# Forty expert weighings on GpSimd begin one group earlier, behind a read-out instead of behind a semaphore

## The reference

```python
# sub-layer 1, a state-space layer (512 channels, 16 states each)
xb, z = split(rms_norm(x) @ in_proj_w)
xc = silu(causal_conv4(xb) + conv_b)
dt, Bm, Cm = split(xc @ x_proj_w)
dt = softplus(dt @ dt_proj_w + dt_proj_b)
h[t] = exp(dt * A) * h[t-1] + dt * Bm * xc      # per channel and state
y[t] = sum_over_states(h[t] * Cm)
y = ((y + xc * D) * silu(z)) @ out_proj_w + x

# sub-layer 2, a mixture of 16 experts (all computed, 4 weighed per token)
combine = top4_of_16_weights(x @ gate_weight)   # zero for the 12 others
act = silu(x @ gate_proj[e]) * (x @ up_proj[e])
y = sum_over_e((act @ down_proj[e]) * combine[:, e])
```

## Time and profile before

| What | Value |
|---|---|
| median of 3 runs | 2657.78 us (2655.29 to 2659.5) |
| time of the profiled execution | 2660.87 us |
| its span, first to last instruction | 2659.1 us |
| PE busy | 2385.4 us (90%) |
| DVE busy | 2418.0 us (91%) |
| ACT busy | 1606.2 us (60%) |
| POOL busy | 1495.1 us (56%) |
| mean granted TensorE clock | 0.957 |
| weighings L896 | 256, 1275 ns each |
| read-outs L911 | 256, 4529 ns each |

### The profile page before, as it was taken

The page is one execution under the profiler, slowest core; times in us unless marked ns, Lnnn a source line. Parts: engine busy times, 40 slices in busy tenths (PEclk is TensorE's granted clock), DMA queues, the critical chain, the costliest instruction groups (busy, mean ns, idle before and its releaser), DMA issues.

```text
span 2659.1 us, 26874 instructions
## 1 busy us (share of the span) xinstructions
PE 2385.4 (90%) x8416; PEld 1187.2 (45%) x8416; DVE 2418.0 (91%) x3097; ACT 1606.2 (60%) x3186; POOL 1495.1 (56%) x531
## 2 busy tenths in 40 slices
PE   5546899999989999898999989899999989898987
PEld 2112354544545454454545445454544545443554
DVE  4989999999999999999999999999999999999542
ACT  6556566665665666666665666666666665644331
POOL 0555565656555565656666565656656565665521
PEclk9768899999999999999999999999999999998999
DMA  4441433525353352534345253534435353442221
GB/s 144 155 145 50 161 130 116 175 87 188 106 154 119 118 183 88 188 108 151 123 133 166 87 188 111 159 112 138 161 94 181 114 161 100 147 149 84 80 71 58
DMA packets 172762, 344.50 MB, mean 130 GB/s; under 512 B 16044, under 2 KB 81357, under 8 KB 164173
## 3 DMA queue, kind: packets, MB, share of 16 engines
q1 hardware_dynamic: 164700, 334.93, 37.5%
q0 software_dynamic: 7920, 7.87, 2.2%
HBM read 291.35 MB, written 51.38 MB: 129 GB/s over the span
## 4 chain that ended last, share of the span: by engine, by line
PE 64%; DVE 20%; ACT 11%; issue 5%; DMA 1%; POOL 0%; SPq 0%; ACTq 0%; DVEq 0%; POOLq 0%
PE Gp L483 13%; PE MY L501 12%; PE Up L491 12%; DVE hs L1033 10%; PE FP L408 7%; PE Y L515 6%; DVE hs L1019 5%; PE FP L446 4%; PE FP L420 3%; PE FP L428 2%; ACT dA L591 2%; ACT XB L684 1%; ACT L591 1%; PE Y L512 1%; DVE th L1148 1%
## 5 line engine op out<-in xcount | busy, mean ns | idle before, releaser
L911 POOL TENSOR_TENSOR hs<-hs,Cb 128x2048 f32<-128x2048 f32 x256 | 1159.5, 4529 | 174.9 <-DVE hs L1019 174.9
L591 ACT ACTIVATE dA<-dtr,A 128x512 f32<-128x512 f32 x1024 | 696.7, 688 | 603.2 <-DVE hs L1033 601.8
L896 POOL TENSOR_TENSOR th<-th,cmb 128x512 f32<-128x512 f32 x256 | 325.5, 1275 | 945.8 <-DVE hs L1019 851.3
L1033 DVE TENSOR_TENSOR_SCAN hs<-dA,carry,hs 128x512 f32<-128x512 f32 x512 | 630.7, 1269 | 13.7 <-ACT dA L591 12.8
L1033 DVE TENSOR_TENSOR_SCAN hs<-dA,hs 128x512 f32<-128x512 f32 x512 | 598.8, 1208 | 37.5 <-ACT dA L591 37.0
L483 PE MATMUL Gp<-x2T,Wgu 128*128 128x512 f32 x1024 | 534.3, 646 | 82.2 <-DVE th L1143 81.6
L1019 DVE TENSOR_TENSOR hs<-dxr,Bb 128x2048 f32<-128x2048 f32 x256 | 587.8, 2296 | 6.9 <-DMA dxr<-dx_d 6.9
L491 PE MATMUL Up<-x2T,Wgu 128*128 128x512 f32 x1024 | 491.6, 603 | 0.0
L501 PE MATMUL MY<-Wdn,th 128*128 128x256 f32 x2048 | 484.4, 380 | 1.6 <-POOL th L896 1.6
L501 PEld LDWEIGHTS MY<-Wdn,th 128*128 128x128 f32 x2048 | 384.3, 190 | 135.1 <-issue 89.8
L483 PEld LDWEIGHTS Gp<-x2T,Wgu 128*128 128x128 f32 x1024 | 183.5, 198 | 420.0 <-issue 275.6
(11 more groups left out here) (168 smaller groups left out, 1798.5 us busy)
## 6 DMA issues: line engine op xcount, KB each, us to landing
dxr<-dx_d SPq DMA_DIRECT2D x128, 512.0 KB, 7.2
dtr<-dt_d SPq DMA_DIRECT2D x64, 1024.0 KB, 5.5
cmb<-cm_d SPq DMA_DIRECT2D x256, 256.0 KB, 3.6
Wdn<-in_w_dn SPq DMA_DIRECT2D x256, 128.0 KB, 3.4
Bb<-bc_d SPq DMA_DIRECT2D x64, 256.0 KB, 3.0
Cb<-bc_d SPq DMA_DIRECT2D x64, 256.0 KB, 3.6
dt_d<-XB SPq DMA_DIRECT2D x15, 1024.0 KB, 4.3
dx_d<-DX SPq DMA_DIRECT2D x15, 1024.0 KB, 5.8
```

The costliest lines, as they stand in the source:

```text
L591: act.activation(dA[h % 2][:, :], dtr[:, M % 2, beta, :], ACT.Exp, scale=A[:, k:k + 1]).then_inc(s_dA, 1)
L896: pool.tensor_tensor(th[:, q % NTH, :], th[:, q % NTH, :], cmb[:, q % 2, :], ALU.mult).then_inc(m_a, 1)
L911: pool.tensor_tensor(hs[:, G % NH, :, :], hs[:, G % NH, :, :], Cb[:, s, :].unsqueeze(1).broadcast_to([P, NBETA, CH]), ALU.mult).then_inc(s ...
L1033: dve.tensor_tensor_scan(hv, dA[h % 2][:, :], hv, first, ALU.mult, ALU.add).then_inc(s_h, 1)
```

## The change

Three groups, 6, 10 and 13, get a second look at the weighing, in periods up to 14. In them the weighing of the expert of group `G - 1` is written behind `read_out(G - 1)`, and the group behind (7, 11 or 14) then has none. That is one weighing in period 1 (group 13) and three in each of periods 2 to 14, forty in all.

```diff
+WEIGH_EARLY = (6, 10, 13)
...
                 if 0 <= G < NGRP:
                     pool.wait_ge(s_u, G + 1)
-                for q in experts_at(G - 2):
-                    weigh(q)
+                if g - 1 not in WEIGH_EARLY or p >= NC - 1:
+                    for q in experts_at(G - 2):
+                        weigh(q)
                 if 0 <= G - 1 < NGRP:
                     read_out(G - 1)
+                if g in WEIGH_EARLY and p < NC - 1:
+                    for q in experts_at(G - 1):
+                        weigh(q)
```

## The result

| What | Before | After |
|---|---|---|
| median of the runs | 2658.5 us (2655.29 to 2659.5, 4 runs) | 2688.86 us (2688.25 to 2689.88, 4 runs) |
| ratio, 95% interval | | 1.0117 [1.0102, 1.0131] |
| span of the profiled execution | 2659.1 us | 2688.1 us |
| mean granted TensorE clock | 0.957 | 0.952 |
| PE, DVE busy | 2385.4, 2418.0 us | 2400.4, 2437.9 us |

The account below looks back on a forecast made before the run. The chain gave PE 64% and POOL 0%, turning to DVE and ACT in groups 10 to 13. Direct 18.2 us plus 6.8 for clock falls made 25 on 2660.87, or 2686; 2682 us for the median, range 2662 to 2693.

Parts of the forecast that it names:

- L956 held in group 6: DVE's first `p_scale2` instruction in group 6 waits for the weighing, paying 0.84 us and delaying `inputs` of group 7.
- group 10, even and odd: In group 10 the weighing holds `f_dx`, on the chain: 0.43 us more in even periods, 0.84 in odd.
- group 12, even: In even periods `inputs` of group 12 no longer meets a read-out's tail, saving 0.11 us on the chain.
- direct sum: Costs over seven even and six odd periods, less the group 12 gain: 8.1 + 10.1 = 18.2 us.
- falls of the clock: After PE's idle time at period ends, 4.5 more drops of TensorE's clock at 1.5 us each: 7 us.
- What DVE meets: A DVE instruction begun during a weighing pays the weighing's end, less its own start, less 0.13 us.
- the clock falls in nearly every period: Rival: TensorE's clock drops at all thirteen period ends, 14 us on top of 18.2, giving 2690 us; chance 0.15.
- PE itself is hardly touched by it before group 10: Group 6's delay of 0.84 us costs PE only some 0.1 to 0.2 at `gate` of group 7.
- `f_dx` comes at about +8.15 and might win: Rival: in group 10 `f_dx` starts before the weighing and is not held; 2665 us, chance 0.23 in some or all periods.
- 0.2 us even: If `f_dx` goes first, group 6's delay costs about 0.2 us per even period, 0.5 per odd: 4.4 us.
- Faster: Rival: at period ends the clock drops vanish, saving 7 us, and DVE collisions are small; 2654 us, chance 0.05.
- nothing moves: Rival: the weighing might wait for `cmb` or `expert_up` and start late, so no effect; chance 0.07.

Follow-up runs that it names:

- e3: Only the weighing of group 13 moved early, against the kernel before; 2657.38 us, ratio 0.9996.
- e10: Kernel before with only group 13's weighing moved, plus four matmuls of zeros on PE at the end of group 13; 2651.39 us, ratio 0.9977.
- e4: Kernel after the change plus four matmuls of zeros on PE at the end of group 13 of periods 2 to 14; 2668.07 us.
- e5: Kernel before the change plus four matmuls of zeros on PE at the end of group 13 of periods 2 to 14; 2652.08 us.
- e6: Kernel before, no weighing moved, with DVE writing part of the inputs of group 11 twice (1.24 us more); 2687.47 us.
- e1: Only the weighing of group 6 moved early, against the kernel before; 2674.13 us, ratio 1.0061.
- e11: Kernel before with group 6's weighing moved, ACT's cast of `z1` in group 7 between its decays, four matmuls of zeros ending group 13; 2651.77 us.
- e9: Kernel before with four matmuls of zeros at the end of group 13 and six more in group 11 ahead of `gate`; 2651.69 us.

## Why the prediction was right, and which step of it failed

| Step | Predicted | Measured |
|---|---|---|
| L956 held in group 6 | about 1.0 us, group + 0.84 | 0.99 us, group + 0.85 |
| group 10, even and odd | + 0.43, + 0.84 | + 0.45, + 0.84 |
| `f_dx` ends at | + 11.51 | + 11.51 and + 11.50 |
| group 12, even | - 0.11 | - 0.12 |
| group 13 | 0 | 0 (e3, e10) |
| direct cost of a period, even and odd | 1.16, 1.68 us | 0.96, 1.78 us (e4, e5) |
| direct sum | 18.2 us | 17.5 us (e4 less e5) |
| falls of the clock | 4.5 more, 6.8 us | 8 more, 11.7 us |

- *What DVE meets.* The price (end of the weighing, less the start on DVE, less 0.13) held at all three kinds of place: 0.96 - 0.13 = 0.83 for L961 against 0.85 paid, 0.73 - 0.13 = 0.60 against 0.61 for `f_dx` in the even period, 0.98 - 0.13 = 0.85 against 0.86 in the odd one. By the full overlap each would have been 0.13 more. Only the forecast of `f_dx` itself, "3 to 3.5 us", was too high for the even periods, where it took 2.88, because it started at +8.63. And the direct cost of a period was off by 0.20 and 0.10 in opposite directions: the shorter group 15, which I had put off the chain, makes even periods shorter by 0.14 us, and most of that comes back in group 5 of the odd ones (10.04 us in e5, 10.15 in e4).
- *The term that was mis-sized is TensorE's clock.* I took the middle between four falls and all, 6.8 us, with no row that spoke for the middle; it was all twelve that lie within the sum (I had counted thirteen places), and 11.7 us. The rival "the clock falls in nearly every period", to which I gave 0.15, is what came: it gave 2690, and 2688.86 is closer to that than to my 2682. That the time lies in the range is owed to the direct part, and to a range drawn wide enough for all falls. "Nothing in the rows favours a fall" was true of the rows that I had read, but e6 shows that a delay on DVE was enough. The size of one fall, 1.51 us, was about right (19.1 / 12 = 1.6).
- *The step that failed is "PE itself is hardly touched by it before group 10".* I compared PE's `gate` of group 7 alone, and it is late by 0.17 us, as said. But `f_x`, behind `gate` and `up`, needs the PSUM bank that ACT empties behind both decays, and PE is late by 0.64 us there (e1), of which e11 leaves 0.17. It did no harm to the sum, because I counted group 10 from its own start. It did make the rival wrong in which `f_dx` comes at about +8.15 and might win: with PE and ACT late too, DVE still waited 0.66 us in group 10 and `f_dx` came at +8.63. And its "0.2 us even" for the delay of group 6 alone was 0.69.
- *Faster* and *nothing moves* had nothing on their side: all forty weighings started within 0.1 us of the end of their read-out.

## What to carry to other kernels

Work that fits into an engine's idle time can still cost time: ask which instructions of the neighbouring engine run in those very tenths of a microsecond, and whether they are on the chain. When an instruction is delayed, follow each buffer that its successors empty, not only the next wait on each engine. And where the profile shows a granted clock that falls only sometimes behind the same idle time, price the all-falls case as fully possible, and try a few matmuls of zeros in the idle time before anything else: here they take 7.4 us off periods 2 to 14 of the kernel before, and 19.1 us off those of the kernel after.

## What the hardware showed that I had not expected

- Four matmuls of zeros, 1.89 us long in the profile, cut PE's idle time from 2.92 to 1.20 us and removed all falls at the periods' ends, 4 of 4 before and 12 of 12 after. A fall that lasted 3.4 us had cost about 1.6 us (19.1 / 12), nearly the half of it that a PE busy throughout loses at half the clock; a fall of the clock in group 11 cost nothing (e9).
- The same idle time, 2.8 to 2.9 us, is followed by a granted clock of 1.00 in some periods and of 0.50 in others, and the share of the latter goes from 4 of 12 to 12 of 12 when 1.24 us of DVE work is added in group 11 (e6).
- Memsets on POOL, one every 0.56 us, that only write SBUF hold a DVE `TENSOR_SCALAR` of four columns (0.55 instead of 0.17 us) but not a `TENSOR_TENSOR` of 2048 columns with two SBUF inputs (2.27 us, as alone).
